# Second attention: six of eight heads masked on VectorE after the exponential instead of on TensorE before it

## The reference

```python
e = jnp.einsum('whqd,whkd->whqk', q, k)
e = jnp.where(e >= 0, e, ALPHA * e)                       # ALPHA = 0.2
attn = jax.nn.softmax(jnp.where(adj[:, None] > 0, e, NEG), axis=-1)
h = jnp.einsum('whqk,whkd->whqd', attn, v)
```

## Time and profile before

| | before |
|---|---|
| runs, median (lowest to highest) | 3390.03 us (3389.32 to 3403.08) |
| profiled execution, device time | 3399.72 us |
| span of its trace | 3397.9 us |
| busy: PE, DVE, ACT, POOL | 3133.1, 2351.7, 2013.3, 1316.1 us |
| TensorE clock granted, mean | 0.976 |

### The profile page before, as it was taken

One profiled execution on the slowest core, in us unless ns is written; L12 is line 12 of the kernel. 1 busy time (PEld: TensorE's weight loads), 2 busy tenths in 40 slices (PEclk: granted clock), 3 DMA queues, 4 the chain that ended last, 5 costly groups with the idle time before them and its releaser, 6 DMA issues. The chain is left out here.

```text
span 3397.9 us, 82395 instructions
## 1 busy us (share of the span) xinstructions
PE 3133.1 (92%) x28999; PEld 2105.6 (62%) x29189; DVE 2351.7 (69%) x6791; ACT 2013.3 (59%) x3726; POOL 1316.1 (39%) x1252
## 2 busy tenths in 40 slices
PE   5999999999999949999999949999999999999996
PEld 3666666666666526666666726766666666666664
DVE  5888888888888835555555546776676767676773
ACT  2666565656555535566555516666666666666664
POOL 0455554555455523444434411333333333333333
PEclk9999999999999969999999969999999999999998
DMA  3444444444444311111111133444444444444431
GB/s 117 136 133 135 139 137 130 134 139 137 128 134 141 92 66 38 50 51 51 50 39 50 38 108 114 135 130 126 127 126 127 126 126 126 127 128 128 133 119 48
DMA packets 291112, 366.77 MB, mean 108 GB/s; under 512 B 31712, under 2 KB 199520, under 8 KB 290656
## 3 DMA queue, kind: packets, MB, share of 16 engines
q1 hardware_dynamic: 289216, 359.25, 34.6%
q10 hardware_dynamic: 1440, 1.65, 0.2%
HBM read 242.29 MB, written 118.49 MB: 106 GB/s over the span
## 5 line engine op out<-in xcount | busy, mean ns | idle before, releaser
L1821 ACT ACTIVATE b_prob<-b_score_t 128x512 f32<-128x512 f32 x512 | 304.4, 595 | 407.5 <-PE b_score_t L2098 403.5
L2011 DVE CUSTOM_DVE_ANT_0 b_junk<-b_score,b_mask 128x256 bf16<-128x256 f32 x1024 | 390.7, 419 | 206.1 <-issue 201.7
L2434 DVE TENSOR_TENSOR f_gl<-f_act,f_gh 128x512 f16<-128x512 f32 x256 | 244.8, 957 | 294.5 <-ACT f_act L2364 294.5
L1888 POOL TENSOR_TENSOR b_nw_root<-b_nw_var,b_minus_halves 128x2 f32<-128x2 f32 x128 | 90.0, 703 | 878.1 <-DVE b_nw_neg_mean L1961 878.1
L1366 DVE TENSOR_TENSOR a_linked<-a_prob,a_mask 128x1024 f32<-128x1024 f32 x256 | 361.1, 1411 | 2.8 <-ACT a_prob L1193 2.7
L2359 ACT ACTIVATE f_gh<-f_up,f_b 128x512 f16<-128x512 f32 x256 | 175.8, 687 | 284.9 <-PE f_up L2475 284.8
L1193 ACT ACTIVATE a_prob<-a_score_t 128x1024 f32<-128x1024 f32 x256 | 259.7, 1014 | 113.5 <-PE a_score_t L1444 100.8
L1359 DVE TENSOR_REDUCE a_neg_max<-a_score 128x4 f32<-128x1024 f32 x256 | 307.6, 1201 | 2.0 <-PE a_score L1457 2.0
L1827 ACT ACTIVATE b_score_t<-b_score_t 128x512 f32<-128x512 f32 x512 | 303.1, 592 | 0.3 <-PE b_score_t L2107 0.3
L2473 PE MATMUL f_down<-f_w,f_gh 128*128 128x256 f16 x1024 | 279.7, 273 | 1.0 <-DVE f_gl L2434 1.0
L2475 PE MATMUL f_down<-f_w,f_gl 128*128 128x256 f16 x1024 | 279.7, 273 | 0.0
(11 more groups left out here) (232 smaller groups left out, 8959.4 us busy)
## 6 DMA issues: line engine op xcount, KB each, us to landing
a_stack<-qk_scratch SPq DMA_DIRECT2D x384, 128.0 KB, 2.8
b_stack<-qk_scratch SPq DMA_DIRECT2D x384, 128.0 KB, 3.0
qk_scratch<-a_qk SPq DMA_DIRECT2D x64, 512.0 KB, 2.8
qk_scratch<-b_qk SPq DMA_DIRECT2D x64, 512.0 KB, 2.9
a_x_sb<-x_t SPq DMA_DIRECT2D x64, 256.0 KB, 3.3
a_adj_sb<-adj_t SPq DMA_DIRECT2D x64, 256.0 KB, 3.4
a_res<-x_nodes SPq DMA_DIRECT2D x64, 256.0 KB, 3.0
after_attention<-a_z_out SPq DMA_DIRECT2D x64, 256.0 KB, 2.8
```

What stands on the lines that cost most here:

```text
L1821: nc.scalar.activation(prob[:, he], score_t[s][:].rearrange("p t n -> p (t n)"), ACT.Exp, scale=ALPHA).then_inc(exp_done, 1)
L2011: last = nc.vector.tensor_tensor_reduce(junk[:, s, it], score[s][:, it], mask[:, i, it], -1.0, 3e38, ALU.add, ALU.min, neg_max[:, i, col:c ...
L2434: nc.vector.tensor_tensor(gl[:, bu[1] % 2, f], act32[:, f % 2], gh[:, bu[1] % 2, f], ALU.subtract).then_inc(low_done, 1)
```

## The change

Six heads (all but 3 and 7) no longer get the matmul with `far` before the exponential. In its place VectorE, one slot after the exponential, sets `prob` to `min(far < 0.5, prob)`: 1 stays an upper bound where a key is seen, and 0 is put where it is not. The exponential gets a bias of -1, so that what is kept lies below 1. Heads 3 and 7 keep the matmul. `values` also waits for the cuts. Moved: `any` from VectorE to ScalarE (a Sign in place of a minimum, in slot 1 and ahead of `xh` in ScalarE's order), and `zero_q` from VectorE to GpSimd (slot 4, first in GpSimd's order). `cut` is the first thing of its slot on VectorE. With `AT["cut"] = 30`, the cuts of heads 0, 1, 2, 4, 5, 6 fall into slots 6, 7, 0, 2, 3, 4.

```diff
+    DIRECT = (3, 7)
+    CUT = tuple(h for h in range(H) if h not in DIRECT)
+    CUTS = len(CUT)
-  ... "ST": 28, "relu": 28, "add": 29, "exp": 29, "values": 33, ...
+  ... "ST": 28, "relu": 28, "add": 29, "exp": 29, "cut": 30, "values": 33, ...
 # ScalarE
                         nc.scalar.activation(prob[:, he], score_t[s][:]..., ACT.Exp,
-                                             scale=ALPHA).then_inc(exp_done, 1)
+                                             scale=ALPHA, bias=minus_one[:]).then_inc(exp_done, 1)
+                    if ba := due(t, h, "any"):          # behind exp, relu, evac, q_hi/k_hi; ahead of xh
+                        i = ba[1] % 2
+                        act.wait_ge(counted, count(ba, 1, 1))
+                        if exists(back(ba, 2)):
+                            act.wait_ge(q_zeroed, count(back(ba, 2), 1, 1))
+                            act.wait_ge(far_ready, count(back(ba, 2), 1, 1))
+                        nc.scalar.activation(any_link[:, i], back_bank[:, 0:N], ACT.Sign).then_inc(any_ready, 1)
 # GpSimd, first in the step
+                    if bp := due(t, h, "zero_q"):
+                        pool.wait_ge(any_ready, count(bp, 1, 1))
+                        pool.wait_ge(qk_low, count(bp, 2, 1))
+                        ...
+                        nc.gpsimd.tensor_tensor(parts, parts, any_link[:, i]..., ALU.mult).then_inc(q_zeroed, 1)
 # GpSimd, ahead of far
+                        if (n := after(back(ba, RING), CUTS, CUTS)) is not None:
+                            pool.wait_ge(cut_done, n)
 # VectorE, first in the step; its "any" and "zero_q" are taken out
+                    if (one := head_due(t, h, "cut")) and one[1] in CUT:
+                        be, he = one
+                        dve.wait_ge(exp_done, count(be, H, he + 1))
+                        if he == CUT[0]:
+                            dve.wait_ge(far_ready, count(be, 1, 1))
+                        head = prob[:, he].rearrange("p (t n) -> p t n", t=NT)
+                        nc.vector.scalar_tensor_tensor(out=head, in0=far[:, be[1] % RING], scalar=0.5, in1=head,
+                                                       op0=ALU.is_lt, op1=ALU.min).then_inc(cut_done, 1)
 # TensorE, add
-                            pe.wait_ge(far_ready, count(be, 1, 1))
-                        nc.tensor.matmul(score_t[s][:]..., far_ident[:], far[:, r4]...)
+                        if he in DIRECT:
+                            pe.wait_ge(far_ready, count(be, 1, 1))
+                            nc.tensor.matmul(score_t[s][:]..., far_ident[:], far[:, r4]...)
 # TensorE, values
                         pe.wait_ge(exp_done, count(bv, H, HQ * (c + 1)))
+                        pe.wait_ge(cut_done, cuts_of(bv, HQ * c + HQ - 1))
```

More of the change, by code:

```diff
@@ L1559, in attention_second @@
     HALVES = 4
+    DIRECT = (3, 7)
+    CUT = tuple(h for h in range(H) if h not in DIRECT)
+    CUTS = len(CUT)
     AT = {"load": 4, "load_adj": 4, "xT": 8, "xh": 9, "xl": 9, "q": 10, "q_hi": 11, "q_lo": 11, "linked": 8, "k": 12, "k_hi": 13, "k_lo": 13,
           "count": 9, "any": 9, "v": 14, "v_out": 15, "zero_q": 12, "far": 10, "store_qk": 13, "mask": 16, "S": 17, "max": 17,
-          "offset": 24, "turn_max": 25, "max_rows": 26, "store_m": 26, "ST": 28, "relu": 28, "add": 29, "exp": 29, "values": 33, "res": 45,
+          "offset": 24, "turn_max": 25, "max_rows": 26, "store_m": 26, "ST": 28, "relu": 28, "add": 29, "exp": 29, "cut": 30, "values": 33, "res": 45,
           "evac": 40, "turn_sum": 40, "rinv": 41, "turn_heads": 43, "hs": 43, "stats0": 44, "z1": 45, "turn_z": 46, "hh": 46, "hl": 47,
@@ L1587, in half_due, with cuts_of @@
         return None
+    def cuts_of(b, h):
+        return count(b, CUTS, sum(k <= h for k in CUT))
     def head_count(b, h, k=0):
@@ L1653, in attention_second @@
         nw = [norm_scratch(ctx, nc, f"{L}nw{i}", NT) for i in range(2)]
+        minus_one = sb("minus_one", [P, 1], F32)
         touch = sb("touch", [P, 4, 1], F32)
@@ L1700, in attention_second @@
         exp_done = sem("exp_done")
+        cut_done = sem("cut_done")
         values_done = sem("values_done")
@@ L1893, in step @@
                 for h in range(H):
+                    if bp := due(t, h, "zero_q"):
+                        i = bp[1] % 2
+                        pool.wait_ge(any_ready, count(bp, 1, 1))
+                        pool.wait_ge(qk_low, count(bp, 2, 1))
+                        parts = qk[:, i, 0:2].rearrange("p k (c n) -> p (k c) n", c=DC)
+                        nc.gpsimd.tensor_tensor(parts, parts, any_link[:, i].unsqueeze(1).to_broadcast([P, 2 * DC, N]),
+                                                ALU.mult).then_inc(q_zeroed, 1)
                     if bg := due(t, h, "stats0"):
@@ L1922, in _ @@
             nc.vector.memset(ones[:], 1.0)
+            nc.vector.memset(minus_one[:], -1.0)
             nc.vector.memset(offset[:], 0.0)
@@ L1964, in step @@
                 for h in range(H):
+                    if (one := head_due(t, h, "cut")) and one[1] in CUT:
[4 more added lines that the diff above has]
+                        head = prob[:, he].rearrange("p (t n) -> p t n", t=NT)
+                        nc.vector.scalar_tensor_tensor(out=head, in0=far[:, be[1] % RING], scalar=0.5, in1=head, op0=ALU.is_lt,
+                                                       op1=ALU.min).then_inc(cut_done, 1)
                     if bf := due(t, h, "hl"):
@@ L1981, in step @@
                                              sums_t[:, N:2 * N].rearrange("p (t a r) -> p t a r", t=NT, a=HQ)[:, :, :, 0:DC]).then_inc(rinv_ready, 1)
[L1982 to L1988, removed]
                     if bm := due(t, h, "max_rows"):
@@ L2044, in step @@
                             nc.vector.tensor_tensor(qk[:, i, 2 * j + 1], proj[:], qk[:, i, 2 * j], ALU.subtract).then_inc(qk_low, 1)
[L2045 to L2051, removed]
                     if ba := due(t, h, "linked"):
@@ L2093, in step @@
                             pe.wait_ge(max_loaded[r4], uses(be, RING) * 16)
+                        if he in DIRECT:
                             pe.wait_ge(far_ready, count(be, 1, 1))
-                        nc.tensor.matmul(score_t[s][:].rearrange("p t n -> p (t n)"), far_ident[:], far[:, r4].rearrange("p t n -> p (t n)"),
-                                         start=False, stop=False, skip_group_check=True)
+                            nc.tensor.matmul(score_t[s][:].rearrange("p t n -> p (t n)"), far_ident[:], far[:, r4].rearrange("p t n -> p (t n)"),
+                                             start=False, stop=False, skip_group_check=True)
                         for jt in range(NT):
```

## The result

The changed kernel takes 3447.95 us (median of 4 runs, 3444.11 to 3455.97) against 3390.88 (4 runs, 3389.32 to 3403.08): 57 us or 1.6% slower, ratio 1.016, 95% interval 1.0132 to 1.0187. Forecast were 3424 us (+34), a range of 3355 to 3470, and "slower" with a chance of 0.61. The profiled execution took 3455.97 us, 56 more than that of before.

What follows compares the result with a forecast made beforehand. The bound was taken to be a loop through VectorE's queue and the DMA transfers, not TensorE. +0.63 up to `k_lo`, less up to 0.12 after it, taken as +0.56 x 60 = 34 us, gave 3424; range 3355 to 3470.

Steps and rivals of the forecast that it cites:

- The loop through VectorE and the transfers: Second attention: each period runs from first-head score through VectorE's queue to `k_lo`, then store and loads; 20.92 us a period.
- Far matmuls: TensorE: six a batch removed, 84 us over 64 batches; only those on the limiting chain count, 0.22 in slot 5.
- part one: First-head score to end of `k_lo`, mean 11.59 us before; forecast to put `k_lo`'s start 0.63 later.
- Cuts of slots 2 and 3: VectorE between `xl` and `q_lo`: two cuts add 2 x 0.60, `xl` gains 0.16, so `q_lo` starts at 7.39 instead of 6.35.
- From `q_lo` to `k_lo` 4.10: Later of two ways: TensorE and ScalarE 4.10 against VectorE 4.01; `k_lo` starts at 11.49 instead of 10.86.
- Part two: End of `k_lo` to next first-head score, mean 9.33 before, set by transfers; forecast gain at most 0.12 a period.
- Third rival, contention: Slot 4: GpSimd's `zero_q` starts before VectorE's cut, which waits 2.3 us; 3556, or 3468 at a third of periods; chance 0.10.
- The sum: Whole loop: +0.56 a period, between +0.51 and +0.63, times 60 periods, 34 us.
- a sign of being right: Mean period 21.4 to 21.6, `q_lo` 7.3 to 7.6, `k_lo` 11.3 to 11.8, k waiting about 1.2, TensorE under 90%.

Runs made afterwards that it cites:

- idle_slots: Changed kernel with cuts of heads 0, 1, 2 only (slots 6, 7, 0), far matmul for the others: 3381.4 us, 0.9975 of the kernel before.
- busy_slots: Changed kernel with cuts of heads 4, 5, 6 only (slots 2, 3, 4), far matmul for the others: 3449.4 us, 1.0176 of the kernel before.
- keep_far: Changed kernel with all its cuts and the far matmul kept for all eight heads: 3450.9 us, 1.0183 of the kernel before.
- moves_only: Kernel before with only `any` moved to ScalarE and `zero_q` to GpSimd; no cut, no bias: 3382.9 us, 0.9982 of the kernel before.
- no_cuts: Changed kernel without its six cuts, so six heads stay unmasked: 3357.3 us, 0.990 of the kernel before.
- pad_pe: Changed kernel with 20 small matmuls on TensorE before its loops, shifting its loop code: 3437.3 us, 1.0139 of the kernel before.
- zero_back: Changed kernel with `zero_q` back on VectorE in slot 4: 3482.2 us, 1.026 of the kernel before.

## Why the prediction was right, and where it fell short

1. *The loop through VectorE and the transfers bounds the kernel, not TensorE.* Right for the changed kernel, and shown by idle_slots against busy_slots, and by keep_far. For the kernel before it is half of it: moves_only shows VectorE's queue and the branch over TensorE and ScalarE of nearly equal length there.
2. *Far matmuls: 84 us taken, nearly all beside the loop; 0.22 in part one.* Right: keep_far puts `k_lo` 0.24 later. "Worth nothing" for those of slots 2 and 3 holds beside the cuts only: without cuts, k starts 0.25 earlier when they are gone (no_cuts against moves_only). All that the far matmuls bring is some 14 us beside the cuts (keep_far against pad_pe) and some 26 without them (no_cuts against moves_only, the bias counted in).
3. *Cuts of slots 2 and 3: 2 x 0.60 ahead of `q_lo`, 0.16 gained at `xl`.* `q_lo` +1.13 instead of +1.04. The cuts were 0.60 from start to start; `xl` gained only 0.06 on the mean.
4. *From `q_lo` to `k_lo` 4.10, by the branch through TensorE and ScalarE.* 4.23: the bias operand, costed at "a few ns" from no row, takes 90 on that branch. Mis-sized, by 0.07 to 0.09. zero_back shows that VectorE's branch is close behind.
5. *Part two: between -0.12 and 0.* In the 50 ordinary periods it fell by 0.23 (9.09 to 8.86), more than the sum allowed. It was not the matmuls that did it: keep_far, which has all of them, stands at 8.84; what did is open. In the five at the back edge it rose by 3.7 (11.9 to 15.6), which is 18.6 us over the 55 periods, 0.34 each, and +0.15 over all. This term was missing: I had taken the long DMA waits of up to 12.8 as given, without seeing that they are the loop's back edge and depend on the code. By pad_pe some 11 of the 57 us are of this kind (7 to 13, by ratios and by traces) and say nothing about the change.
6. *Third rival, contention.* VectorE won against `zero_q` in slot 4, as expected; `zero_q` took 2.58 (it takes 2.12 in idle_slots, where no cut stands in slot 4; the 2.34 of the sum was too long) and was done at 2750.31, before `k_lo`. No cut of slots 2 to 4 took over 0.79. The lock was there all the same: the cut of slot 6 started at 2751.77 behind `affine` of 2751.50 and took 1.55, and `affine`'s next instruction took 1.60 instead of 1.27 behind a cut. The rule of the Trainium skill, "SBUF — State Buffer", "Who interferes with whom", holds in this trace: in 170 of 171 cases a cut that started with more than 0.15 us of a GpSimd instruction left ended 0.54 to 0.56 us after that instruction's end, as here (2753.32 behind 2752.77). It mattered little, since the long waits struck where VectorE had time and `far` held the cut of slot 4 by 0.09 only.
7. *The sum: +0.56 a period.* +0.96: part one +0.82 instead of +0.63, the ordinary periods' part two -0.20 instead of about -0.06, and the back edge +0.34. The mean period, 21.88, lies outside the 21.4 to 21.6 named as a sign of being right; `q_lo`, `k_lo`, the wait of k and TensorE's share lie inside theirs. The direction and the place were right, the size was 60% of it. That the ordinary periods alone rose by 0.60, nearly the forecast, is luck: two misses of opposite sign cancel there. And the range, 3355 to 3470, reached from faster to slower, so that lying inside it says little.

## What to carry to other kernels

Ask of an instruction that is moved between engines in which slot it lands, and whether the loop that bounds the kernel goes through the receiving engine there: three cuts in place of three matmuls changed next to nothing in slots 6, 7 and 0, and took 68 us more in slots 2, 3 and 4, with the shorter durations. The busiest engine need not be the bound: at 96% TensorE was not, and eighty-four microseconds of its work were worth about 14 beside the cuts and 26 without them. Before a small loss or gain is believed, look at the loop's back edge: here a shift of the code alone made about 11 us, and whether the clock fell there 1.4 us each time.

## What the runs showed of the hardware

- An activation with a bias read from a 128x1 tile took 684 ns instead of 594 for 128x512 from PSUM.
- A VectorE instruction with two SBUF inputs that started beside a GpSimd `tensor_tensor` ended 0.54 to 0.56 us after that one's end, and took up to 1.55 us instead of 0.68; the other way round `zero_q` on GpSimd took 2.58 us beside a cut and 2.12 without.
- After a stop of TensorE at the back edge the granted clock fell in some periods and not in others: behind two of the five stops of the kernel before, behind all five of the changed one. There it was 0.50 from 2650.0 to 2653.5, so that TensorE's work ran at the lower of its two levels, 1.2 GHz. Such a period was some 1.4 us longer (24.4 against 23.0 before).
- The same program with 20 small matmuls more ahead of its loops ran 10.6 us faster (7 by the ratios); a second stop of TensorE, of 1.4 to 2.0 us in each back-edge period, was no longer there.
